# A fused macaron block (MoE, attention, MoE) on one core: the row maxima are split earlier on VectorE, and a batch's first two score units go ahead of its neighbour's closing value products

## The reference

```python
# x: (8, 512, 128), 16 heads of 8; ffn is a mixture of 8 experts, 2 chosen for each row
x = x + 0.5 * ffn(layernorm(x))
x = x + attention(layernorm(x))
x = x + 0.5 * ffn(layernorm(x))

def attention(x):
    q = (x @ q_w + q_b) ...            # (8, 16, 512, 8)
    k, v = (x @ kv_w + kv_b) ...
    att = q @ k.T / sqrt(8) + slope[head] * (key - query)
    att = softmax(where(key <= query, att, -inf))
    return (att @ v) @ o_w + o_b
```

## Time and profile before

| what | before |
|---|---|
| device time, median of 3 executions | 814.48 us (810.95 to 814.7) |
| span of the profiled execution (first to last instruction) | 816.6 us |
| PE busy | 669.3 us, 82% |
| PEld / DVE / ACT / POOL busy | 502.2 / 564.3 / 413.6 / 490.0 us |
| chain that ended last, by engine | PE 52%, DVE 22%, issue 7%, DMA 5%, POOL 4%, ACT 4%, SPq 4% |

### The profile page before, as it was taken

One profiled execution on the slowest core, in us unless ns is written; L12 is line 12 of the kernel. 1 busy time (PEld: TensorE's weight loads), 2 busy tenths in 40 slices (PEclk: granted clock), 3 DMA queues, 4 the chain that ended last, 5 costly groups with the idle time before them and its releaser, 6 DMA issues.

```text
span 816.6 us, 17042 instructions
## 1 busy us (share of the span) xinstructions
PE 669.3 (82%) x5103; PEld 502.2 (62%) x5103; DVE 564.3 (69%) x2041; ACT 413.6 (51%) x931; POOL 490.0 (60%) x596
## 2 busy tenths in 40 slices
PE   1657979988958998989989999999898789988840
PEld 0547969978934655656655556575553449987840
DVE  3678779988559766767768677587666225897674
ACT  2345426646601664555655556566544566855620
POOL 2567772466026663768868778364653467777772
PEclk9999999999979999999999999999999899999975
DMA  8816688743563223032140230311301216443465
GB/s 227 249 51 158 167 196 204 158 118 87 134 178 96 60 50 75 1 101 64 29 120 18 71 94 2 86 39 36 89 1 46 77 33 171 141 113 91 109 209 172
DMA packets 89829, 84.13 MB, mean 103 GB/s; under 512 B 14561, under 2 KB 72556, under 8 KB 89580
## 3 DMA queue, kind: packets, MB, share of 16 engines
q1 hardware_dynamic: 74472, 57.51, 27.8%
q0 software_dynamic: 8800, 19.72, 8.0%
q10 hardware_dynamic: 6468, 5.83, 3.0%
HBM read 43.87 MB, written 31.13 MB: 92 GB/s over the span
## 4 chain that ended last, share of the span: by engine, by line
PE 52%; DVE 22%; issue 7%; DMA 5%; POOL 4%; ACT 4%; SPq 4%; ACTq 2%; DVEq 0%; POOLq 0%
PE bank L2371 9%; PE bank L2299 8%; PE bank L2346 8%; PE bank L2215 5%; PE bank L2201 5%; PE pair L2142 3%; DVE mx L1851 2%; DVE mx L1853 2%; POOL y_rows L915 2%; SPq L566 2%; PE pair L2394 1%; PE bank L2175 1%; ACT arena L1271 1%; DMA arena<-z_rows 1%; DMA y_rows<-arena 1%
## 5 line engine op out<-in xcount | busy, mean ns | idle before, releaser
L1271 ACT ACTIVATE arena<-bank 128x512 f32<-128x512 f32 x320 | 186.1, 601 | 174.6 <-PE bank L2346 172.7
L946 POOL TENSOR_SCALAR_AFFINE_SELECT arena<-arena 128x256 f32<-128x256 f32 (+1 forms) x192 | 94.6, 517 | 125.5 <-ACT arena L1271 125.4
L2299 PE MATMUL bank<-kZ,qT 128*128 128x512 f32 (+3 forms) x512 | 148.9, 358 | 20.3 <-DMA kZ<-oT 9.4
L2346 PE MATMUL bank<-qT,kZ 128*128 128x512 f32 (+3 forms) x512 | 156.9, 378 | 2.6 <-DMA qT<-mT_zero 1.9
L2299 PEld LDWEIGHTS bank<-kZ,qT 128*128 128x128 f32 x512 | 87.5, 196 | 67.9 <-DVE mx L1854 19.2
L1206 ACT ACTIVATE arena<-bank,hidden_bias 128x128 f32<-128x128 f32 x320 | 91.3, 370 | 69.7 <-PE bank L2201 69.0
L1851 DVE TENSOR_REDUCE mx<-bank 128x1 f32<-128x512 f32 x128 | 87.2, 681 | 51.8 <-PE bank L2273 51.6
L2371 PE MATMUL bank<-arena,vA 128*9 128x512 f32 (+3 forms) x1024 | 95.0, 451 | 15.8 <-issue 6.1
L2346 PEld LDWEIGHTS bank<-qT,kZ 128*128 128x128 f32 x512 | 85.3, 198 | 25.1 <-ACT arena L1271 11.2
L2215 PE MATMUL bank<-w_rot,arena 128*128 x640 | 97.8, 290 | 2.1 <-ACT arena L1206 2.1
L856 POOL DMA_INDIRECT sums<-y_rows,y_place x56 | 55.1, 984 | 73.6 <-DMA y_rows<-arena 58.8
(11 more groups left out here) (276 smaller groups left out, 1232.0 us busy)
## 6 DMA issues: line engine op xcount, KB each, us to landing
arena<-z_rows SPq DMA_DIRECT2D x160, 66.0 KB
qT<-parts SPq DMA_DIRECT2D x42, 128.0 KB
kZ<-parts SPq DMA_DIRECT2D x168, 32.0 KB
y_rows<-arena SPq DMA_DIRECT2D x20, 264.0 KB, 3.5
kZ<-bias_k_r SPq DMA_DIRECT2D x8, 512.0 KB
beside_kZ<-y_rows SPq DMA_DIRECT2D x7, 528.0 KB, 7.4
z_rows<-in_spare SPq DMA_DIRECT2D x4, 528.0 KB, 6.5
z_rows<-in_spare SPq DMA_DIRECT2D x32, 66.0 KB
```

The lines of the kernel that those rows point to most:

```text
L946: g_.affine_select(out=cut, in_=cut, compare_op=ALU.is_ge, fill=0.0, base=0, pattern=[[0, 2], [0, blocks], [1, P]], channel_multiplier=-1) ...
L1271: a_(dst, src, ACT.Exp).then_inc(exp_ok.sem, 1)
L2299: mm(outp, qT[u][:, t, query_tile * P:(query_tile + 1) * P], kZ[u][:, h, 0:keys], start=start, stop=False, skip_group_check=(kind != "full"))
L2346: return mm(outp, kZ[u][:, h, lo:lo + P], qT[u][:, t, lo:SEQ], start=start, stop=True, skip_group_check=(kind != "full"))
```

## The change

Three things move, and no instruction is added or removed.

- VectorE's `maxima(b + 1)` stands behind the reductions of unit 34's place instead of behind the whole loop, so ahead of `gate_place`. ScalarE's copy of the transposed maxima moves from behind exponential 37 to behind exponential 36 (`AT_MAX`). TensorE's transposes stay where they were.
- TensorE: `values` of the batch before, group 3, kb = 0 and 1, stood ahead of unit 0 and now stand behind unit 1; kb = 2 stood behind unit 0 and now stands behind unit 2; kb = 3 stood behind unit 1 and now stands behind unit 3.
- ScalarE's `o_evac` of that group moves from behind exponential 2 to behind exponential 3.

```diff
-AT_MAX_T, AT_MAX = 36, 37
+AT_MAXIMA, AT_MAX_T, AT_MAX = 34, 36, 36
+AT_LAST_VALUES = (1, 1, 2, 3)
+AT_LAST_O = 3
@@ scalar, batch
                 for n in range(N_UNITS):
                     exp_(b, n)
-                    if n == 2 and not first:
+                    if n == AT_LAST_O and not first:
                         o_evac(b - 1, 3)
@@ vector, batch
                     if later >= 1:
                         for a in beside(n):
                             reduce_(b + 1, a)
-                if later >= 1:
-                    maxima(b + 1)
+                        if n == AT_MAXIMA:
+                            maxima(b + 1)
@@ tensor, batch
-                if later >= 1:
-                    for a in beside(0):
-                        scores_for_max(b + 1, 1 - u, a)
-                if not first:
-                    for kb in range(NT // 2):
-                        values(b - 1, 1 - u, NG - 1, kb)
                 for n in range(N_UNITS):
                     t, i = divmod(n, UNITS)
-                    if later >= 1 and n:
+                    if later >= 1:
                         for a in beside(n):
                             scores_for_max(b + 1, 1 - u, a)
                     scores(b, u, n)
                     if not first:
-                        if n < NT // 2:
-                            values(b - 1, 1 - u, NG - 1, NT // 2 + n)
+                        for kb in range(NT):
+                            if n == AT_LAST_VALUES[kb]:
+                                values(b - 1, 1 - u, NG - 1, kb)
```

## The result

The kernel after took 807.1 us (median of 4 executions, 804.58 to 809.22), the kernel before, on the same chip, 814.6 us (4 executions, 810.95 to 819.76). The ratio is 0.990, with a 95% interval of 0.986 to 0.994: about 1% faster. The forecast was 807.0 us. Run again, twelve times, it took 808.33 us, ratio 0.992 (0.988 to 0.995).

A forecast was written before the change was run, and what follows sets the result against it. TensorE, busy 82%, sets the pace over most of the attention, GpSimd's queue in batches 2 to 4. Gains 4.4 + 1.0 + 0.7 + 1.4 = 7.5 us off the median 814.48 give 807.0 us, range 803.0 to 812.5.

The forecast's parts named there:

- GpSimd's queue ends batches 2 to 4: From exponential 39 to `values(b, 0, 0)` GpSimd never idles, so each of three boundaries gains 1.47 us, 4.4 in all.
- The split is ready in time, the port costs nothing: VectorE's split ends near 412.05, TensorE needs it at 413.16; a port shared with GpSimd might add up to 1.4 us, taken as 0.
- A new wait of 0.57 us for the operands: At 2 to 3, TensorE's first `scores_for_max` unit waits for `kZ`, landing 2.54 us after its issue ends, at 415.87.
- the bound from below: If the operands land earlier than assumed, TensorE gains up to 1.6 us at a boundary.
- Unit 0 waits 0.07 us: At 2 to 3, unit 0 starts at 417.82, the maxima's DMA taking 3.40 us from start of issue to unit 0.
- its slower rival: Unit 0 waits long for the maxima's DMA, deciding from about 4.1 us of landing on; up to 820.5 us, chance 0.07.
- the sign: Forecast wrong if unit 0's wait for its DMA is over 1 us in the middle boundaries.
- Batches 5 and 6 go by the front, 1.0 and 0.7: At 4 to 5 and 5 to 6 TensorE's front decides; gains of 1.0 and 0.7 us.
- Batch 7, 1.4: At 6 to 7 exponential 4 comes 1.4 us earlier, opening GpSimd's queue to the select TensorE awaits: 1.4 us gained.
- The clock, no stretch added: TensorE's new 0.57 us pause is shorter than the 1.24 removed, so no slow-clock stretch is added or removed.
- the bound of 1.5 us: Allowance for TensorE's clock: 1.5 us either way, a slow stretch costing 1.48 us over 16 value products.
- the last three rows of the table: Boundaries 4 to 5, 5 to 6 and 6 to 7, with predicted gains of 1.0, 0.7 and 1.4 us.

The follow-up runs named there:

- the order alone: Only TensorE's order and `o_evac` changed against the kernel before, split and copy where they were: 818.89 us, ratio 1.002.
- the split alone: Only VectorE's `maxima` split moved earlier against the kernel before: 807.45 us, ratio 0.989.
- the sends moved: Kernel before with four of GpSimd's sends moved behind the selects of unit 9, nothing else: 805.54 us, ratio 0.986.
- the best kernel: Changed kernel with GpSimd's four sends behind the selects of unit 9 and SyncE's 256 KB store behind the maxima's DMA: 789.69 us, ratio 0.970 to before.

## Why the prediction was right, point by point

- *GpSimd's queue ends batches 2 to 4, so they gain what exponential 39 gains.* Right for batches 3 and 4, and shown by three runs: the order alone (more waits, same period there), the split alone (whole gain), the sends moved (1.44 us a period from nothing else). 1.47 us predicted, 1.58 and 1.52 found. Wrong for batch 2, where GpSimd idled 2.47 us for exponential 4. The wait left at `values(b, 0, 0)` was 1.05 and 1.14 us, not 0.5: with 1.58 us gained and a slack of 1.34, TensorE reached it 1.29 us earlier at 2 to 3, twice the 0.66 that was worked out.
- *The split is ready in time, the port costs nothing.* Right: the split's copy took 0.195 us in all eight places. A cost came elsewhere, on `gate_place`'s copy (below). At 2 to 3 that copy ends at 410.58 and TensorE's ranks at 410.45, so next to nothing of it shows.
- *A new wait of 0.57 us for the operands.* Wrong. It was 0.41 at 1 to 2, 0.28 at 4 to 5, else none. At 1 to 2 unit 0 of `scores_for_max` came 1.69 us after the end of the issue (354.41 + 2.80 to 358.90), not the 2.54 of the earlier trace rows; in the best kernel it came 2.74 after it. One row was no measure of this landing; the bound from below that I gave, up to 1.6 us at the front, was the better half.
- *Unit 0 waits 0.07 us.* The term most mis-sized: 1.62, 1.09, 1.03, 0.46 and 0.20 us from 1 to 2 on. The landing took 4.76, 3.82, 3.75 and 3.59 us at the first four, not 3.40: at the earlier trace rows no store stood ahead of it, here one does. The prediction named the mechanism as its slower rival, with 4.1 us as the point from which it decides, and at 1 to 2 it was passed; there unit 0 came 1.20 us later than at 2 to 3, and that is part of the loss. At 2 to 3 and 3 to 4 it cost nothing, because GpSimd's queue lay behind it; its price had been worked out on TensorE's front alone. I had also written that I would be wrong if unit 0 waited over 1 us in the middle. It did, and the forecast stood: the sign was badly chosen, since a wait that GpSimd's queue covers doesn't count.
- *Batches 5 and 6 go by the front, 1.0 and 0.7.* Right that TensorE's front decides, but by another way, and mis-sized. It acts through exponential 4, for which GpSimd idled 2.01 and 1.23 us; four sends and the select of unit 9 follow, and for these TensorE waits 0.68 us at both `values(b, 0, 0)` (put down to an exponential, as in the earlier trace rows). They gained 1.41 and 1.20. The prediction followed that way for batch 7 only.
- *Batch 7, 1.4.* Right in the way, through exponential 4, but 2.26. The slow stretch came again, as predicted (2.73 us for the 16 value products).
- *The clock, no stretch added.* Wrong at one boundary, 1 to 2, where the slow stretch took 1.60 us, near the bound of 1.5 us that I gave it. The boundary fell 2.4 us short of its forecast; the rest is the late landing of the maxima, 1.20 us at unit 0, less some 0.3 us that GpSimd's queue still covered.

So 7.06 us came for 7.5: terms too small by 1.8 (the last three rows of the table) and 0.2 (2 to 3, 3 to 4) stand against the 2.4 of 1 to 2. That the sum is so close is partly luck. So is that the median came out at 807.1 us: the sum leaves out what lies ahead of the attention and behind it. The mechanism in the middle isn't luck.

## What to carry to other kernels

A wait that an engine shows is worth only what no other chain fixes: look downstream for the next wait of the same engine, and follow its releaser's queue back to where it last idled. If that queue is fed by an event that the change brings forward, count the event's gain; if not, count nothing, and look whether something in the queue can stand later. Then ask up to which delay that queue still covers the new waits: at 1 to 2 it no longer did, and there the change lost. A small DMA with a waiter behind it should be issued ahead of large ones on the same queue: here that took 0.9 us off a landing, though its worth in time was not clear of the noise.

## What the runs showed of the hardware

- The copy in `gate_place` (128 x 8), moved beside GpSimd's selects, took 0.63 us in six of six places, before 0.16. This view of the copy's line in both kernels (ns min/median/max), the first of before, the second of after:

```profile
L1616 DVE COPY w<-fixed x6: 160/161/161, 358.6 to 620.8; 128x8 int32<-128x8 int32 x6
```

```profile
L1618 DVE COPY w<-fixed x6: 625/628/628, 355.5 to 612.9; 128x8 int32<-128x8 int32 x6
```

  GpSimd's three selects ran beside it, from 409.47 to 410.92. The 0.63 us agree with the rule of the Trainium skill, "SBUF — State Buffer", section "Who interferes with whom", which the prediction held against the split's copy; it struck the neighbour. No row shows the port itself.
- The same 64 KB DMA was awaited until 2.9 to 4.9 us after its issue. With the 256 KB store issued 0.5 us ahead of it, it was 3.6 to 4.9 us; 0.8 to 1.4 us ahead, 2.9 to 3.8; 2.4 to 3.0 us ahead (the order alone), 3.05 to 3.23; behind it, 2.9. Ahead of the first batch, with no store near, it was 3.2 to 3.9, so the store isn't all of it.
- At 1 to 2 the lower clock came after waits of 0.41 and 1.62 us, and in other kernels after 1.43 and 0.80 or one of 1.90, but not in the fastest kernel after one wait of 2.00 us, nor with the order only, after 1.25 and 1.30 us. What tips it, these runs don't show.
